# Two recurrences of 512 channels: the bias goes into the PSUM accumulators by ScalarE writes, in place of a two-row matmul in each step

## The reference, cut to what matters

```
xw = jnp.einsum('ntd,dh->nth', x, Wx) + b          # L1
next_h = jnp.tanh(xw_t + prev_h @ Wh)

gate = jax.nn.sigmoid(h @ Wh.T + z_t @ Wz.T + b)   # L3
h_new = jnp.tanh(h * leak + gate * z_t)
```

## Time and profile before

| | |
|---|---|
| runs | 2130.57, 2132.01 and 2131.35 us: median 2131.35 us |
| profiled execution | 2128.01 us, its span 2126.1 us, mean granted TensorE clock 0.983 |
| busy in the span | PE 2037.1 us (96%), PEld 1210.5 (57%), DVE 1048.1 (49%), ACT 769.9 (36%), POOL 197.9 (9%) |
| bias matmuls in the span | 88 in rnn, 120 in leaky |
| rnn | from the start to about 303 us; its first projection matmul at 26.60 |
| leaky | from about 1741 us to the end; rough chunks to about 1811 us, fine warm-up chunks to about 1905 |

### The profile page before, as it was taken

How to read it: one execution, slowest core, us unless ns; L and a number is a source line. 1 busy time by engine, 2 the same in 40 slices (tenths; PEclk the granted TensorE clock), 3 DMA queues, 4 the chain that set the end, 5 groups by cost and what they waited for, 6 DMA issues and landing times. The chain is left out here.

```text
span 2126.1 us, 45095 instructions
## 1 busy us (share of the span) xinstructions
PE 2037.1 (96%) x17984; PEld 1210.5 (57%) x17984; DVE 1048.1 (49%) x2208; ACT 769.9 (36%) x1668; POOL 197.9 (9%) x215
## 2 busy tenths in 40 slices
PE   7999979999999997999999999999999987999997
PEld 4999964444444443444444444444444445998886
DVE  5466646644764544111111175454524326777777
ACT  3333335422121333444344443122211126555554
POOL 0000000000073000111111120110201000000000
PEclk9999999999999998999999999999999989999999
DMA  7023337764252424999999764220302320001001
GB/s 279 2 100 122 123 110 188 220 189 139 100 198 68 153 98 144 223 206 204 202 199 207 170 198 166 78 90 12 133 15 90 109 80 1 3 3 41 39 39 42
DMA packets 242859, 254.29 MB, mean 120 GB/s; under 512 B 194088, under 2 KB 194222, under 8 KB 236048
## 3 DMA queue, kind: packets, MB, share of 16 engines
q1 hardware_dynamic: 229760, 216.60, 35.1%
q0 software_dynamic: 12944, 35.51, 6.3%
HBM read 150.00 MB, written 56.43 MB: 97 GB/s over the span
## 5 line engine op out<-in xcount | busy, mean ns | idle before, releaser
L936 PE MATMUL sh_p<-xh,arena 128*128 128x512 f16 x2048 | 613.5, 381 | 13.2 <-DVE xl L1158 7.3
L936 PE MATMUL sh_p<-xl,arena 128*128 128x512 f16 x1024 | 390.7, 382 | 0.0
L936 PEld LDWEIGHTS sh_p<-xh,arena 128*128 128x128 f16 x2048 | 200.7, 98 | 258.8 <-issue 16.0
L951 PE MATMUL sh_p<-sh_h_hi,arena 128*128 128x512 f16 x1024 | 306.6, 381 | 0.0
L1084 ACT ACTIVATE sh_sig<-sh_p,fac 128x512 f32<-128x512 f32 x128 | 87.9, 687 | 393.8 <-PE sh_p L936 390.0
L1518 PE MATMUL ro_pf<-arena,ro_xt 128*128 x852 | 197.6, 382 | 13.0 <-DMA ro_xt<-xh 11.2
L1574 DVE SCALAR_TENSOR_TENSOR ro_hs<-xres,fac,ro_hs 128x512 f16<-128x512 f32 x71 | 53.3, 751 | 309.3 <-ACT ro_hs L1561 309.3
L1364 DVE SCALAR_TENSOR_TENSOR sh_half_h<-sh_sig,sh_p 128x512 f32<-128x512 f32 x128 | 87.8, 686 | 236.1 <-ACT sh_sig L1084 236.1
L1090 ACT CAST sh_h_hi<-sh_full_h 128x512 f16<-128x512 f32 x128 | 79.0, 618 | 328.8 <-DVE sh_full_h L1367 328.8
L1518 PE MATMUL ro_py<-arena,ro_ht 128*128 x852 | 195.4, 379 | 0.7 <-DMA ro_ht<-ro_hs 0.7
L951 PE MATMUL sh_p<-sh_h_lo,arena 128*128 128x512 f16 x512 | 195.0, 381 | 0.0
(11 more groups left out here) (261 smaller groups left out, 3157.7 us busy)
## 6 DMA issues: line engine op xcount, KB each, us to landing
stage<-in_shared_w SPq DMA_DIRECT2D x29, 768.0 KB, 4.9
routed_rows<-xres SPq DMA_DIRECT2D x71, 256.0 KB, 2.6
stage<-in_norms_r SPq DMA_DIRECT2D x16, 1024.0 KB, 4.9
stage<-in_routed_w SPq DMA_DIRECT2D x16, 1024.0 KB, 4.8
stage<-in_norms SPq DMA_DIRECT2D x14, 1024.0 KB, 5.2
arena<-x SPq DMA_DIRECT2D x12, 1024.0 KB, 5.4
rnn_xs<-in_x SPq DMA_DIRECT2D x8, 1024.0 KB, 17.8
x<-xres SPq DMA_DIRECT2D x16, 512.0 KB, 2.7
```

Of the source, the lines that this page charges most:

```text
L936: mm = nc.tensor.matmul(p1[u % P1][:], arena[:, w:w + P], x[slot(gl)][:, :, k, :], start=(j == 0), stop=(j == 3 * KD - 1))
L951: mm = nc.tensor.matmul(p2[m][:], arena[:, w:w + P], h[n % 2][:], start=(i == 0 and j == 0), stop=(i == HID - 1 and j == 2))
```

## The change

- The bias is loaded as a column, `bias` [128, 4], one element for each channel, and multiplied with the weights' scale by one VectorE operation. `b2`, `b_lo`, `ones16`, the split of the bias into two parts, the DMA of its low part and one memset go away.
- The bias matmul at the end of `bulk` goes away (88 in rnn, 120 in leaky). No projection matmul has `start=True` any more: all add to what stands in PSUM.
- `set_bias(p, bank)`, a new ScalarE instruction, writes the bias, repeated over 256 columns for two blocks (512 elements in each partition), into one bank of acc[p]. `bulk` waits for it (`bias_set`) at m = 0 and m = 2.
- The first four writes (both banks of both accumulators) come once at the start, in `set_first`. After that each chunk has two: in step j = 0 the second bank of the other accumulator (not in chunk 0), and in step j = 3 the first bank of its own one. Both stand behind the step's tanh and ahead of the cast of x. `all_read` waits beforehand until ScalarE itself has read the bank for the last time.
- Four matmuls of 512 columns, `mark`, write into all four banks at the start with `start=True`, so that later matmuls add there; ScalarE then overwrites what they wrote. In rnn they use w1 (f32) and stand behind the first `gate_rows`, in leaky wr_hi (f16), at the very start.

```diff
             @block.gpsimd
             def _(pool):
-                nc.gpsimd.memset(ones16[:], 2.0 ** 10).then_inc(zeroed, 1)
...
-                    pool.dma_start(b2[1:2, :], b_lo[:]).then_inc(b_ready, 16)
...
+                def mark(w):
+
+                    for i in range(2):
+                        for pair in (slice(0, 2), slice(2, 4)):
+                            nc.tensor.matmul(acc[i][:, pair, :], w[:, 0, 0:P], w[:, 0, :], start=True, stop=True).then_inc(marked, 1)
+
+                if not gate:
+                    mark(wr_hi)
                 if gate:
                     pe.wait_ge(cond_in, 48)
                     pe.wait_ge(w1_in, 16)
                     gate_rows(cond, w1)
+                    mark(w1)
                     pe.wait_ge(row_out, 1)
                     gate_turns()
...
+                    if m % 2 == 0:
+                        pe.wait_ge(bias_set, q * 2 + m // 2 + 1)
                     cols = slice(m * P, (m + 1) * P)
                     for k in range(KD):
                         for w, x in (((wx_hi, x_hi),) if rough else ((wx_hi, x_hi), (wx_lo, x_hi), (wx_hi, x_lo))):
-                            nc.tensor.matmul(acc[p][:, m, :], w[:, k, cols], x[p][:, k, :], start=(m % 2 == 0 and k == 0 and x is x_hi and w is wx_hi),
-                                             stop=False, skip_group_check=True)
-                    mm = nc.tensor.matmul(acc[p][:, m, :], b2[:, cols], ones16[:], start=False, stop=False, skip_group_check=True)
+                            mm = nc.tensor.matmul(acc[p][:, m, :], w[:, k, cols], x[p][:, k, :], start=False, stop=False, skip_group_check=True)
...
+                def set_bias(p, bank):
+
+                    pair = slice(2 * bank, 2 * bank + 2)
+                    nc.scalar.activation(acc[p][:, pair, :], bias[:, pair].unsqueeze(2).broadcast_to([P, 2, CW]), ACT.Copy).then_inc(bias_set, 1)
+
+                def all_read(q, s):
+
+                    if leaky:
+                        act.wait_ge(g_ready, s * parts)
+                    else:
+                        act.wait_ge(hi_ready, (s + 1) * parts)
+                        if not rough_chunk(q):
+                            act.wait_ge(h32_ready, (s - ROUGH * CHUNK_STEPS + 1) * parts)
...
                     nc.scalar.activation(wr_hi[:], wraw[:, 0], ACT.Copy, scale=scale[:, 0:1]).then_inc(wr_hi_ready, 1)
+                    act.wait_ge(b_ready, 1)
+                    set_first()
                     act.wait_ge(wx_in, 16)
...
+                        if j == 0 and not (isinstance(q, int) and q == 0):
+                            all_read(q, s)
+                            set_bias(1 - p, 1)
+                        if j == CHUNK_STEPS - 1:
+                            all_read(q, s + 1)
+                            set_bias(p, 0)
                         if ahead is not None:
                             if j == 0:
                                 act.wait_ge(bulk_done, q + 1)
                             split(q + 2, p, ahead, j)
```

More of the change, by code:

```diff
@@ L70, in scan_layer @@
             wx_hi, wx_lo = sb("wx_hi", [P, KD, D], F32R), sb("wx_lo", [P, KD, D], F32R)
-            brow, bs = sb("brow", [1, D]), sb("bs", [1, D])
-            b_lo, b2 = sb("b_lo", [1, D], F16), sb("b2", [2, D], F16)
+            bias = sb("bias", [P, KD])
             scale, inv_scale = sb("scale", [P, 1]), sb("inv_scale", [P, 1])
@@ L75, in scan_layer @@
             xs, x_hi, x_lo, hist, xo = (ready[n] for n in ("xs", "x_hi", "x_lo", "hist", "xo"))
-            wr_hi, wr_lo, wx_hi, wx_lo, b2, inv_scale, decay = (ready[n] for n in ("wr_hi", "wr_lo", "wx_hi", "wx_lo", "b2", "inv_scale", "decay"))
-        ones16 = sb("ones16", [2, CW], F16)
+            wr_hi, wr_lo, wx_hi, wx_lo, bias, inv_scale, decay = (ready[n] for n in ("wr_hi", "wr_lo", "wx_hi", "wx_lo", "bias", "inv_scale", "decay"))
         mx = sb("mx", [P, 4])
@@ L175, in _ @@
                     sp.dma_start(w2[:], gate["w2"]).then_inc(w2_in, 16)
-                    sp.dma_start(brow[:], src["b"]).then_inc(b_in, 16)
+                    sp.dma_start(bias[:], src["b"]).then_inc(b_in, 16)
                     sp.dma_start(wraw[:, 1], src["wx"]).then_inc(wx_in, 16)
@@ L335, in _, with set_first @@
             def _(act):
+                def set_bias(p, bank):
[8 more added lines that the diff above has]
+                            act.wait_ge(h32_ready, (s - ROUGH * CHUNK_STEPS + 1) * parts)
+                def set_first():
+                    act.wait_ge(marked, 4)
+                    for i in range(2):
+                        for bank in range(2):
+                            set_bias(i, bank)
                 if gate:
@@ L483, in _ @@
                     dve.wait_ge(b_in, 16)
[L484 to L486 removed]
+                    nc.vector.tensor_scalar(bias[:], bias[:], scale[:, 0:1], None, ALU.mult).then_inc(b_ready, 1)
                     dve.wait_ge(lt_mm, 1)
@@ L490, in _ @@
                     nc.vector.tensor_copy(grow[:], pg[0][0:BATCH, :]).then_inc(row_out, 1)
-                dve.wait_ge(zeroed, 4 if leaky else 3)
+                dve.wait_ge(zeroed, 3 if leaky else 2)
                 link(nc.vector.tensor_copy(h_hi[:, :, 0:BATCH], cond[:]))
@@ L660, in next_scan @@
     return {"xs": xs, "x_hi": x_hi, "x_lo": x_lo, "hist": hist, "xo": xo, "wr_hi": wr_hi, "wr_lo": wr_lo, "wx_hi": wx_hi, "wx_lo": wx_lo,
-            "b2": keep["b2"], "inv_scale": keep["lk_inv"], "decay": keep["decay"], "x_loaded": keep["lk_loaded"], "loaded": [g for g, _ in EARLY]}
+            "bias": keep["bias"], "inv_scale": keep["lk_inv"], "decay": keep["decay"], "x_loaded": keep["lk_loaded"], "loaded": [g for g, _ in EARLY]}
 def shared_part(nc, src, part, keep, x_in, x_out, dram):
@@ L750, in shared_part @@
             scan = keep["scan"]
-            brow, b_lo, b2, decay, lk_scale, lk_mx = (keep[n] for n in ("brow", "b_lo", "b2", "decay", "lk_scale", "lk_mx"))
+            bias, decay, lk_scale, lk_mx = (keep[n] for n in ("bias", "decay", "lk_scale", "lk_mx"))
             wr_raw, wx_raw = (stage[q % 2][:].rearrange("p (k n) -> p k n", k=KD) for q in (LOADED, LOADED + 1))
-            b_in, wr_hi_ready, wx_hi_ready, b_lo_ready, split_done = (sem(n) for n in ("b_in", "wr_hi_ready", "wx_hi_ready", "b_lo_ready", "split_done"))
+            b_in, wr_hi_ready, wx_hi_ready, split_done = (sem(n) for n in ("b_in", "wr_hi_ready", "wx_hi_ready", "split_done"))
         CHOSEN = 13
@@ L861, in _ @@
                     load_old(0)
-                    sp.dma_start(brow[:], src["l3_b"]).then_inc(b_in, 16)
+                    sp.dma_start(bias[:], src["l3_b"]).then_inc(b_in, 16)
                     sp.dma_start(decay[:], src["l3_alpha"]).then_inc(b_in, 16)
@@ L1601, in build @@
                 "ids": sm("ids", [P, TILES], I32), "token_of": sm("token_of", [P, SLOT_TILES], I32), "owner": sm("owner", [1, SLOT_TILES], I32),
-                "brow": sm("brow", [1, D]), "b_lo": sm("b_lo", [1, D], F16), "b2": sm("b2", [2, D], F16), "decay": sm("decay", [P, KD]),
+                "bias": sm("lk_bias", [P, KD]), "decay": sm("decay", [P, KD]),
                 "lk_scale": sm("lk_scale", [P, 1]), "lk_inv": sm("lk_inv", [P, 1]), "lk_mx": sm("lk_mx", [P, 4]),
@@ L1650, in layout @@
         "w2": rows(a["L0_cond_W2"].T), "b2": column(a["L0_cond_b2"]),
-        "l1_wx": rows(a["L1_cond_Wx"]), "l1_wr": rows(a["L1_cond_Wh"]), "l1_b": a["L1_cond_b"].reshape(1, D),
-        "l3_wr": rows(w3[:, :D].T), "l3_wx": rows(w3[:, D:].T), "l3_b": a["L3_cond_b"].reshape(1, D),
+        "l1_wx": rows(a["L1_cond_Wx"]), "l1_wr": rows(a["L1_cond_Wh"]), "l1_b": column(a["L1_cond_b"]),
+        "l3_wr": rows(w3[:, :D].T), "l3_wx": rows(w3[:, D:].T), "l3_b": column(a["L3_cond_b"]),
         "l3_alpha": column(a["L3_cond_alpha"]),
```

15 lines of the change are left out of this document (3 added, 12 removed).

## The result

| | before | changed |
|---|---|---|
| median of the runs | 2130.96 us (2128.48 to 2132.01) | 2097.57 us (2096.83 to 2099.57) |
| profiled execution, its span | 2128.01, 2126.1 | 2099.57, 2097.1 |

The two profiled executions stand 28.4 us apart, where my sum said 27.2. That is a better match than the sum deserves: terms are off on both sides, and the first trace of the kernel before is unusual in its clock. Its mean granted clock is 0.983, where 36 later executions of the same kernel in two other groups lie between 0.971 and 0.980. Its time of 2128.01 us is an ordinary one among them.

What follows compares the result with a forecast made beforehand. TensorE was taken to bound the fine steps of rnn and leaky, the chain ACT, DVE, ACT, PE with a full ScalarE leaky's rough steps. Seven terms summed to -27.2 us, giving a 2104 us median, range 2099 to 2116.

Steps and rivals of the forecast that it cites:

- Term 1: rnn's 76 steps that carry a fine projection: each gains 0.30, the write lying in ScalarE's idle time; -22.8 us.
- Term 2: rnn's 8 steps with rough projection: between -2.4 and +1 us, taken as 0.
- Term 3: Start of rnn: marking products and four writes delay the second sigmoid by 3.3, four bias matmuls leave, -1.2; +2.1 us.
- Term 4: Start of leaky: four marking matmuls and one write add 2.2, four bias matmuls leave, -1.2; +1.0 us.
- Term 5: leaky's 28 rough steps: no gain from the bias matmul, 13 writes delay a sigmoid by 0.40 each; +5.2 us.
- Terms 6 and 7: leaky's fine steps: seven warm-up chunks at -0.51, -3.6 us; full round, 14 chunks at -0.58 plus chunk 14, -9.1 us.
- The gap did not stay: Rival: the switch of type keeps the gap, 0.21 gained per step; sum -17.8, 2113.5 us; chance 0.20.
- a write is not dear: Rival: a write into an accumulator costs 0.9 us; sum -13.8, 2117.5 us; chance 0.08.
- no slower: Rival: slower than before, with 4.3 us more lost at about 1.3 us a write; chance 0.04.
- A low clock: Rival: a low clock, still faster than before; sitting in a fine stage it would prove the forecast wrong; chance 0.08.
- upper bound of 2116: Slow end of the range: the gap stays and a low stretch comes; 2116 us.
- lower bound: Fast end of the range: writes at 0.4 us and rnn's 8 rough steps gaining; 2099 us.

Runs made afterwards that it cites:

- bias_64_rows: The kernel before with the bias matmul's operands on 64 rows instead of 2; 2129.05 us beside 2129.99.
- bias_128_rows: The kernel before with the bias matmul kept but its operands on 128 rows, the added weight rows zero; 2158.14 us, ratio 0.9852.
- no_bias: The kernel before with the bias matmul taken out and nothing in its place, so the result lacks the bias; 2145.55 us, ratio 0.9784.
- before_third: The kernel before, run again unchanged against itself; 2129.26 us, ratio 0.9994.
- leaky_only: The kernel before with the change in leaky alone, rnn keeping its bias matmul; 2117.93 us, ratio 0.9944.
- writes_doubled: The changed kernel with a second write of the same size, to a spare SBUF tile, behind each write in a step; 2117.59 us, ratio 0.9946.
- after_third: The changed kernel run again, unchanged, against the kernel before; 2096.50 us, ratio 0.9841.
- start_late: rnn with writes, its marks on f16 zeros and first writes behind the second sigmoid; leaky's bias matmul on 128 rows; against the kernel before 2088.65 us, ratio 0.9815.
- rnn_only: The kernel before with the change in rnn alone, leaky keeping its bias matmul; 2169.22 us, ratio 0.9894.

## Why the prediction came out as it did

The mechanism was right: without the 2-row matmul its two neighbours stand 0.12 apart, and in rnn's fine steps the writes are hidden. The forecast of the repeating fine steps was right to 0.05 us, but for the first one of each full-round chunk (3.10, where 3.25 less 0.30 was forecast). What was off are sizes, and nearly all of them in rough steps and starts, where the granted clock has a part.

- **The short matmul keeps loads from running ahead: right, and shown.** 0.29 to 0.30 per step in 73 of the 76 steps; bias_64_rows and bias_128_rows show that the row count alone sets the gap, and their load rows that the load runs ahead with 128 rows only, by 0.11. 64 rows behave as 2 do (0.42), 128 don't (0.24). Why the row count has this effect is in no row.
- **Term 1, -22.8, measured -21.2.** The step from rough to fine waits for x_lo, which comes behind a write and a cast (2.51 became 3.02; 2.41 in no_bias), and two of the last steps are not bound by TensorE alone (3.59 to 3.39, 3.40 to 3.39).
- **Term 2, 0, measured -2.4: mis-sized.** I took the rough steps at 1.36 from one trace. In before_third the first three take 2.30, at a granted clock of 0.50; leaky_only, with the short matmul in rnn, shows 2.30 twice and bias_64_rows 2.31 and 2.06. In all kernels without the short matmul these steps are 1.22 to 1.43 (writes_doubled apart), and the clock is up earlier: 3.5 to 5.0 us behind the first projection matmul in those ten traces, 7.9 to 13.9 in the four with it. The windows of before_third, and then of after_third (busy time of each engine, then the granted clock, here 0.50, 0.50 and 0.93, the DMA share and GB/s):

```profile
31.00:34.00 3.00, 3.00 (x31) 2.33 (x32) 3.00 (x4) 0.77 (x2) 0.00 (x0) 0.50 1.02 406
34.00:37.00 3.00, 3.00 (x33) 2.55 (x31) 2.10 (x7) 0.86 (x3) 0.00 (x0) 0.50 1.05 425
```

```profile
33.40:37.00 3.60, 3.57 (x60) 3.16 (x60) 3.60 (x3) 1.75 (x5) 0.00 (x0) 0.93 1.06 426
```

- **Term 3, +2.1, measured +2.0: right in the sum, by luck.** The second sigmoid ran at 28.06, 27.4 was forecast; over the two traces before and the three after it comes 4.4 later, not 3.3; the marking products alone put gate_turns off from 16.17 to 19.22, by 3.0 where I had 2.2. From it to the first state matmul the time fell from 8.33 to 5.96, by 2.4 and not by 1.2. That is the four bias matmuls again, dearer than I had them for the reason given under term 4. The two errors cancel.
- **Term 4, +1.0, measured -0.2: mis-sized, by the same 1.2.** The mark and the write cost what I said (the projection starts 2.64 after the mark's start). What I had wrong is the price of the four bias matmuls: 0.30 each, which rnn's fine steps show at full clock. At both starts the granted clock is 0.50, and there it is twice that, 0.62. In the kernel before, four projection matmuls with the bias matmul behind them take 1.47 to the next four:

```profile
1742.34 0.39 PE L263 MATMUL leaky_acc<-leaky_ones,b 2*128 2x256 f16 x1
...
1742.66 1.22 PE L261 MATMUL leaky_acc<-leaky_x_hi,leaky_wx_hi 128*128 128x256 f32 x4
...
1743.81 0.39 PE L263 MATMUL leaky_acc<-leaky_ones,b 2*128 2x256 f16 x1
...
1744.13 1.22 PE L261 MATMUL leaky_acc<-leaky_x_hi,leaky_wx_hi 128*128 128x256 f32 x4
```

  In the changed kernel, at the same 0.50, it is 0.85 (all 16 in the 3.75 above), so 0.62 each; with 64 rows it is 1.47 too, and with 128 rows, in start_late, 1.09. The same 20 matmuls of the start take 7.12 from memset to first sigmoid in bias_64_rows, and 4.72, 4.77, 5.78 and 5.78 in the four kernels with 128 rows, where the clock was back at 1.0 before the end in the first two and at 0.50 throughout in the others.
- **Term 5, +5.2, measured +2.0: mis-sized.** A write costs 0.33 and not 0.40 (it takes 0.52 from start to start and the sigmoid follows the cast 0.30 later), so 4.3 at full clock. At half clock plain steps cost 0.1 more in either kernel (2.38 against 2.27), while a step with a write hides it (2.60 at both clocks); and the first step that carries a fine projection, 4.01, 4.12 and 4.40 in three of four traces with the short matmul (at a granted clock of 0.59, 0.56 and 0.50 over the step; 2.87 at 1.0 in the fourth), was 2.71 to 2.72 in all four with single writes there, with the clock back at 1.0. The window of the earlier trace rows, at 0.52, held that step: I took a low clock for a danger to the changed kernel only, and it was a cost of the kernel before. It is not the short matmul's doing alone, for no_bias, which has none, took 3.99 at 0.50.
- **Terms 6 and 7, -3.6 and -9.1, measured -4.0 and -8.4: right.** Chunk ends came at 3.49 and 3.72; the first step of a full-round chunk gained 0.15, not 0.30, so a chunk 0.52 and not 0.58.
- **The rivals.** The gap did not stay; a write is not dear; no slower. A low clock, to which I had given 0.08, did come in leaky's rough stage (0.59 of the full clock where the first trace of before had 0.96), but it put nothing on top of the forecast: the kernel before has a low clock there in other executions (0.68 in before_third and in rnn_only), and the stage came out below the forecast, not above it. The cost of a low stretch that the upper bound of 2116 counts is my estimate, and no run shows it apart. In its place: the same code took 66.70 us for that stage at a clock of 0.96, and 68.27 and 68.7 at 0.68.

So the step that failed is the pricing of the starts and rough stages, read from one trace and, for the bias matmul, from fine steps at full clock. Terms 2, 4 and 5 together came out 6.8 us too high. What the runs showed in their place: with the short matmul rnn's first rough steps take up to 2.31 at a granted clock of 0.50, and without it they are 1.22 to 1.43 (term 2: -2.4, not 0); a bias matmul costs 0.62 and not 0.30 at that clock (term 4: -0.2, not +1.0, and hidden in term 3 by a second sigmoid that came later than forecast); and a write in leaky's rough steps costs 0.33 and not 0.40, while the kernel before loses more there than its first trace shows (term 5: +2.0, not +5.2). Term 1 was 1.6 too favourable, the others came out within 0.7, and so the sum was 5 us short of the -32.2 of the stages. The lower bound took in cheap writes and the 8 rough steps, but nothing for the clock to give back.

What stays open: what decides TensorE's clock in leaky's rough stage. It differs between executions of one code (0.96 and 0.68 in the two traces of before, 0.68 in rnn_only, whose leaky is the same); it is 0.82 with 64 rows and 0.67 without bias. It stood at 0.85 to 0.96 in the four traces with the 128-row matmul there and at 0.58 to 0.67 in the four with single writes. That suggests that writes leave it low, but no_bias, with neither, is low as well, and no run here separates the two.

## To carry to other kernels

A matmul on 2 or 64 rows between ones on 128 cost far more here than its columns: at full clock 0.42 from one neighbour to the other, against 0.12 + 0.12 on 128 rows, and padding its operands with zero rows gave as much as moving the work to another engine, for an edit of two shapes. When work is moved to an engine with room, count what stands in its queue at each place: in rnn's fine steps, bound by TensorE, the move was free, in leaky's rough steps, bound by ScalarE, it cost 0.33 each, and the best version uses both forms. And take lengths of stages with idle TensorE from more than one trace, with the clock beside them, and the price of an instruction from rows at the clock that it will run at.

## What the runs showed of the hardware that I had not expected

- A matmul on 64 rows is as much in the way as one on 2: 0.42 between its neighbours at full clock; on 128 rows 0.24. At a granted clock of 0.50 a group of four projection matmuls and one short one takes 1.47 on 2 or 64 rows, 1.09 on 128 and 0.85 without it.
- TensorE's clock came back sooner in rnn's start where no matmul on 2 or 64 rows stood between the others. In the four traces that have such matmuls there the granted clock rose from 0.50 to 1.0 at 7.9 to 13.9 us behind the first projection matmul, in the ten others at 3.5 to 5.0 behind it. At leaky's start the 16 projection matmuls with 4 short ones between take 7.10 to 7.12 us to the first sigmoid in all four traces that have them, with the granted clock at 0.50 throughout, and 4.72 to 5.78 with 4 on 128 rows. Part of that is the shorter gaps and not the clock, as the two at 5.78 stood at 0.50 too. What the clock goes by was not tested.
- A write into an accumulator takes 0.58 to 0.60 us for 128 x 512, 0.52 from start to start; the second ones, into SBUF, 0.61 to 0.62.
